# A graph layer's last turns reordered, its adjacency chunks kept in DRAM in 7 stripes

## The chip, the cores and the metric

The kernel runs on one core of a Trainium2 chip. The metric is device time in microseconds (us). Five engines work side by side: PE (TensorE: matmuls and transposes), DVE (VectorE), ACT (ScalarE), POOL (GpSimd) and SP (SyncE, which here only issues DMAs). Each runs its own program in order, and they wait on each other through semaphores. SP, ACT and POOL each have a DMA queue; all queues share the core's 16 DMA engines.

## The reference

Two graph layers over 6250 nodes (256 features) and 206250 edges, then a mixture of 8 experts (2 chosen per node). Cut to what matters:

```
norm = ew * rsqrt(deg_out[src] * deg_in[dst] + EPS)
h6   = relu(segment_sum((h5 @ W6)[src] * norm, dst) + b6)      # layer 1
h7   = relu(segment_sum((h6 @ W7)[src] * norm, dst) + b7)      # layer 2
x    = x + h7 @ Wp + bp
x    = x + moe(layernorm(x))      # gelu(xn @ W1[e] + b1[e]) @ W2[e] + b2[e], e = the top 2 of 8
```

The edges come sorted by `dst`.

## The kernel before

**Two ways to sum edges.** Edges are cut into tiles of 128. The first 736 tiles of layer 1 (784 of layer 2) are *dense*: 24 (26) chunks, for each of which an adjacency block of 49 x 128 rows by 134 columns is built in SBUF (`adj`, two buffers of 3283 KB) and multiplied by the whole feature table on PE (L2098, 49 matmuls a chunk). Layer 1 builds each block with DVE (`add_tile`, L1323) and SP stores it to DRAM (`store_chunk`, L763); layer 2 only loads it back (`load_chunk`, L768, for chunks 0 and 1 on ACT's queue, L1906). The DRAM tensor `chunks` holds 128 rows per chunk, one row of 26264 bytes for each partition.

The other tiles come in *groups* of 8, 110 in layer 1 and 104 in layer 2. POOL gathers the 8 x 128 source rows of a group from the layer's table in DRAM with 8 indirect DMAs (L977) into one of 4 ring buffers, and waits with a group until PE has summed the group 4 before it. PE sums a group (`sums`, L2111). After every second group ACT copies the sums (`copy_sums`, L1760), PE aligns them (`combine`, L2124), ACT copies the result (`copy_rows`, L1767), and SP adds the pair of groups to the node sums in DRAM (`store_group`, L740). Ahead of each odd group's `combine`, SP must have loaded one carried row (`carry_row`, L731), which was written by the store before. `store_group(L, n)` is the carried row's load for even n, and the store for odd n.

**Pairs.** Nodes are finished in 25 pairs of 128-row blocks. SP loads the pair's sums (`load_early`, L776), DVE scales them, PE transposes (L2133), ACT does the relu (L1805), PE projects (L2150), ACT scales (`pair_out`, L1814), and in layer 1 SP stores the rows to layer 2's table (`store_table`, L798). POOL begins layer 2's gathers only when all 25 pairs are in that table.

**The last turns of layer 1.** Groups 96 to 109 run in 14 turns (k = 0 to 13) of which each engine does its share in a written order. Pairs 9 to 22 are spread over turns 4 to 11 as 1, 2, 2, 2, 1, 2, 2, 2. In a turn PE does `sums`, dense steps and one-hot builds, all pairs of the turn, then `combine`; SP does the pairs' DMAs and then `store_group`. Pairs 23 and 24 follow behind turn 13. Turn 4 also issues `load_stored`, 2304 KB of the table back into SBUF; ACT issues a chunk store in turn 5 and a chunk load in turn 7.

**Layer 2's slots.** Each slot does one group and a third or a quarter of a chunk. From chunk 8 on every chunk has 4 slots and begins at an even slot, where SP issues the next chunk's load, a carried row of the dense sums, and then the group's carried row. A pair takes 6 slots (stages 0 to 5: transposes and `project`; residual and two normalisations on DVE, `residual_and_norms` L1369; router; places; the list, twice). `pair_starts` (L623) gives every pair its first slot, at least 3 apart; a pair whose rows end in a group can begin no sooner than slot `groups_for(1, b)` (L602). After slot 103 there are no more groups: slots 104 to `SLOTS` - 1 take two expert blocks each (`tail_slot`, L2260; 105 blocks in all), and DVE copies the experts' weights for them (`weights_at`, L1594, L1582) at the head of slots from 104 on. The other blocks follow in a plain loop.

Of the kernel before, what the change touches and what calls it, by code (L numbers as in the profile page):

```python
# [14 lines left out]
P = 128  # L15
# [40 lines left out]
OFFS, CHUNK_OFFS = 16, 32  # L56

# [27 lines left out]
def gnn_moe_kernel(nc, A):  # L85
# [37 lines left out]
    with ExitStack() as ctx:  # L123
# [16 lines left out]
        chunks = nc.dram_tensor("chunks", (ALL * P, XB_ALL * AWID), F32, kind="Internal").ap()  # L140
# [397 lines left out]

        def slice_bounds(i):
            return first_of_step(ZERO_BEHIND[i - 1] + 1) if i else 0, first_of_step(ZERO_BEHIND[i] + 1)  # L540


        LATE_PAIR = LOOP_PAIRS + 1
        TURNS = TAIL - TAIL_FROM - 2
        TAIL_PAIR_COUNT = LATE_PAIR - EARLY_PAIRS
        TAIL_PAIRS = [range(0)] * TAIL_FROM + [range(EARLY_PAIRS + TAIL_PAIR_COUNT * k // TURNS,
                                                     EARLY_PAIRS + TAIL_PAIR_COUNT * (k + 1) // TURNS)
                                               for k in range(TURNS)] + [range(0)] * 2
# [53 lines left out]
        def groups_for(L, b):  # L602
            return min(2 * ceil_div(tiles_before((b + 1) * PT * P) + 2 * TG - G0[L] * TG, 2 * TG), GROUPS[L])
# [71 lines left out]
        def _(sp):  # L675
# [87 lines left out]
            def store_chunk(c):  # L763
                sp.wait_ge(added, chunk_start(c + 1))
                sp.dma_start(chunks[c * P:(c + 1) * P, :], adj[:, c % 2].rearrange("p h w -> p (h w)")
                             ).then_inc(chunk_stored, 16)

            def load_chunk(c):  # L768
                sp.wait_ge(applied[1], SLICES * (c - 1))
                sp.dma_start(adj[:, c % 2].rearrange("p h w -> p (h w)"), chunks[c * P:(c + 1) * P, :]  # L770
                             ).then_inc(chunk_in[c % 2], 16)
# [50 lines left out]
            with sp.If(bad < 1):  # L822
# [39 lines left out]
                for k in range(TAIL):  # L862
                    if k == TAIL_FROM:
# [185 lines left out]
        def _(dve):  # L1049
# [600 lines left out]
            with dve.If(bad < 1):  # L1650
# [39 lines left out]
                for b in range(LATE_PAIR, NPAIR):  # L1690
                    tail_pair(b)
# [43 lines left out]
        def _(act):  # L1735
# [81 lines left out]
            def tail_pairs(pairs):  # L1817
                for b in pairs[:1]:
                    pair_root(b)
                for b in pairs:  # L1820
# [3 lines left out]
                    if b > EARLY_PAIRS:  # L1824
                        pair_out(b - 1)

# [79 lines left out]
            def load_chunk(c):  # L1906
                act.wait_ge(chunk_stored, 16 * (CHUNKS + c + 1))
                act.dma_start(adj[:, c].rearrange("p h w -> p (h w)"), chunks[c * P:(c + 1) * P, :]
# [574 lines left out]
```

## Time and profile before

| | us |
|---|---|
| median of 3 runs | 3170.95 (3157.32 to 3171.85) |
| the profiled execution, its own time | 3166.45 |
| its span, first to last instruction | 3164.5 |
| layer 1's gathers on POOL | 373.4 to 1520.0 |
| layer 2's gathers on POOL | 1555.3 to 2640.3 |
| PE / POOL / DVE busy | 83% / 62% / 60% of the span |

The profile lists for each engine its instructions with start, duration and, in brackets, how long the engine had been idle and what ended that. POOL's busy share leaves out the 0.30 us that it needs between two gathers.

### The profile page before, as it was taken

What the parts mean: (1) busy time and instruction counts of PE and PEld (TensorE: products, weight loads), DVE (VectorE), ACT (ScalarE), POOL (GpSimd) and SP (SyncE); (2) the same over time, 40 slices, a digit from 0 to 9 for tenths busy, and PEclk for the clock granted to TensorE, in tenths of its full rate; (3) what the DMA queues carried; (4) which work ended last, traced back from release to release, by engine and by line L of the source; (5) the groups of instructions that cost most, each with busy time, mean ns of one, the idle gap of its engine ahead of it and who ended that gap; (6) DMA issues with size and microseconds to landing.
All of it is one profiled execution on the core that took longest, in us unless ns stands there. A gap on an engine that the chain in (4) does not pass through costs nothing. (4 is left out here: it accounts for less than half of the span.)

```text
span 3164.5 us, 53882 instructions
## 1 busy us (share of the span) xinstructions
PE 2631.7 (83%) x16919; PEld 2013.0 (64%) x16919; DVE 1911.0 (60%) x6028; ACT 861.5 (27%) x2052; POOL 1963.4 (62%) x1932
## 2 busy tenths in 40 slices
PE   4567479999999999995589988888888875899995
PEld 3456247676667776663466766666666553889984
DVE  9999878888888887864203545455545446522210
ACT  5677611122121222112201100000011001456652
POOL 0000277777777777777477777777777763467763
PEclk8699789999999999997899999899999885999997
DMA  4001355566665655668666766666666663344444
GB/s 129 0 22 43 115 166 181 201 204 203 199 203 193 195 188 191 203 199 276 207 201 226 259 213 213 194 217 215 226 220 221 219 226 93 60 66 71 70 67 115
DMA packets 197506, 530.79 MB, mean 168 GB/s; under 512 B 39338, under 2 KB 129247, under 8 KB 190463
## 3 DMA queue, kind: packets, MB, share of 16 engines
q0 software_dynamic: 102336, 252.47, 30.5%
q1 hardware_dynamic: 92174, 256.65, 22.4%
q10 hardware_dynamic: 2736, 18.48, 1.5%
q8 instruction: 131, 2.15, 0.3%
q14 instruction: 129, 1.05, 0.1%
HBM read 377.61 MB, written 156.24 MB: 169 GB/s over the span
## 5 line engine op out<-in xcount | busy, mean ns | idle before, releaser
L977 POOL DMA_INDIRECT arena<-table,src_i x1712 | 1673.7, 978 | 596.2 <-issue 514.5
L2098 PE MATMUL bank<-arena 128*128 128x257 f32 x4900 | 1246.5, 391 | 3.1 <-ACT zcd L1784 2.4
L2098 PEld LDWEIGHTS bank<-arena 128*128 128x128 f32 x4900 | 901.7, 194 | 202.5 <-issue 83.4
L2083 PE MATMUL bank<-arena 128*128 128x294 bf16 x2352 | 426.2, 295 | 49.6 <-DVE arena L1295 32.3
L1323 DVE TENSOR_TENSOR arena<-arena,bank 128x294 f32 x784 | 357.3, 456 | 176.4 <-PE bank L2083 164.9
L1295 DVE SCALAR_TENSOR_TENSOR arena<-iota_f,arena 128x256 f32<-128x256 f32 x784 | 366.8, 468 | 0.0
L2083 PEld LDWEIGHTS bank<-arena 128*128 128x128 bf16 x2352 | 226.4, 100 | 207.9 <-DVE arena L1323 46.3
L2111 PE MATMUL bank<-arena,s_all 128*32 128x257 f32 x3424 | 246.2, 408 | 75.1 <-DMA arena<-table,src_i 68.4
L1771 ACT COPY arena<-zero 128x2144 f32<-128x2144 f32 (+1 forms) x104 | 156.3, 1533 | 398.3 <-DMA chunks<-arena 335.9
L1003 POOL DMA_INDIRECT acc<-arena x105 | 178.7, 1702 | 126.6 <-ACT arena L1897 97.6
L1294 DVE TENSOR_SCALAR arena<-iota_key,arena 128x294 bf16<-128x294 bf16 x784 | 242.7, 310 | 0.0
L2055 PE MATMUL bank<-arena 128*128 128x150 bf16 x1616 | 152.6, 256 | 107.6 <-DVE arena L1143 72.2
L1582 DVE COPY arena<-arena 128x1024 f32 x105 | 76.2, 733 | 261.9 <-PE bank L2297 245.7
L968 POOL PARTITION_ALL_REDUCE bad_all<-bad_f x1 | 0.4, 380 | 358.4 <-DVE bad_f L1285 358.4
L2055 PEld LDWEIGHTS bank<-arena 128*128 128x128 bf16 x1616 | 132.7, 109 | 128.9 <-DVE arena L1143 107.3
L2297 PE MATMUL bank<-arena 128*128 128x128 f32 x1680 | 211.0, 280 | 0.0
L2306 PE MATMUL bank<-arena 128*128 x840 | 203.1, 384 | 8.8 <-ACT arena L1897 8.8
L2111 PEld LDWEIGHTS bank<-arena,s_all 128*32 128x32 f32 x3424 | 93.5, 114 | 178.6 <-DMA arena<-table,src_i 76.1
L1760 ACT COPY zs<-bank 127x257 f32<-127x257 f32 x107 | 40.1, 375 | 608.2 <-PE bank L2111 607.3
L2297 PEld LDWEIGHTS bank<-arena 128*128 128x128 f32 x1680 | 202.2, 197 | 0.1
L2306 PEld LDWEIGHTS bank<-arena 128*128 128x128 f32 x840 | 153.3, 193 | 28.3 <-issue 10.5
L990 POOL DMA_INDIRECT arena<-rows_x,arena x105 | 109.2, 1040 | 85.1 <-DVE arena L1487 34.0
(238 smaller groups left out, 2678.3 us busy)
## 6 DMA issues: line engine op xcount, KB each, us to landing
chunks<-arena SPq DMA_DIRECT2D x25, 3283.0 KB, 12.7
arena<-chunks SPq DMA_DIRECT2D x24, 3283.0 KB
arena<-table,src_i POOLq DMA_INDIRECT x1712
zsum<-zc SPq DMA_DIRECT2D x107, 128.5 KB, 3.2
zrow<-zsum SPq DMA_DIRECT2D x50, 257.0 KB, 4.7
arena<-in_W ACTq DMA_DIRECT2D x16, 512.0 KB, 16.9
rows_x<-arena SPq DMA_DIRECT2D x25, 264.0 KB
arena<-chunks ACTq DMA_DIRECT2D x2, 3283.0 KB
```

Of the source, the lines that this page charges most:

```text
L977: pool.indirect_dma_start(gat[:, r, j, 0:D], None, table[L], bass.IndirectOffsetOnAxis(ap=src_i[:, col:col + 1], axis=0)).then_inc(gathere ...
L1003: pool.indirect_dma_start(acc, bass.IndirectOffsetOnAxis(ap=row_e[:, j:j + 1], axis=0), ye[:, j % 2], None, compute_op=ALU.add).then_inc(y ...
L1294: dve.tensor_scalar(ohk[:, r], iota_key[:, 0:KEYS], key[:, t:t + 1], None, ALU.is_equal)
L1295: dve.scalar_tensor_tensor(out=words[:, r], in0=bc_mid(iota_f[:, :], 2), scalar=lo_f[:, t:t + 1], in1=bc_in(w_words[:, t], P), op0=ALU.is_ ...
L1323: dve.tensor_tensor(win, win, ps_b[t % len(ps_b)].rearrange("p (h w) -> p h w", w=TW), ALU.add).then_inc(added, 1)
L1771: done = act.copy(adj[:, c % 2, first:first + whole], zero[:, :].unsqueeze(2).broadcast_to([P, whole, AWID]))
L2055: last = pe.matmul(ps_do, oh_lo[:, r, j // TI, :, j % TI], whi[:, r, j // TI, :, :, j % TI].rearrange("p i n -> p (i n)"), start=False, st ...
L2083: last = pe.matmul(ps_b[t % len(ps_b)], halves[:, t % OH_RING, word, :, half], ohk[:, t % OH_RING], start=(i == 0), stop=(i == 2))
L2098: last = pe.matmul(ps_ap, adj[:, c % 2, h, 0:P], xp[:, h], start=(h == 0), stop=(h == XB_ALL - 1))
L2111: last = pe.matmul(ps_seg[q * WIN:(q + 1) * WIN, :], s_mat[:, r, q * HQ + j], gat[:, r, q * HQ + j], start=(j == 0 and not second), stop=( ...
L2297: last = pe.matmul(ps_h[j % 2][:, c], w1_e[:, j % W1_RING, k, c * P:(c + 1) * P], xeT[:, j % 2, k], start=(k == 0), stop=(k == KD - 1))
L2306: last = pe.matmul(ps_y, hs[:, j % 2, c], w2_of(e, c), start=(c == 0), stop=(c == HC - 1))
```

## The change

Four things change.

1. `chunks` in DRAM gets 7 rows of 3752 bytes for each partition of a chunk in place of one of 26264; the same bytes are stored and loaded, each partition in 7 pieces.
2. In the last turns of layer 1 an odd turn's `combine`, `copy_rows` and `store_group` come behind the turn's first pair and no longer behind its last; an even turn's carried row is issued before the pairs.
3. Pair 23 (`LATE_PAIR`) is moved from behind turn 13 into turn 12; its projection comes ahead of the last group's `sums` on PE. One pair, 24, is left behind the last group.
4. For that, `groups_for` asks for 8 tiles of margin where it asked for 16. Layer 2's planner uses the same function. By its formula these first slots move, and the rest stay: pairs 14, 15, 16, 17 from 30, 38, 46, 54 to 28, 36, 44, 52; pair 23 from 104 to 102; pair 24 from 107 to 105. `SLOTS` goes from 113 to 111.

```diff
+STRIPES = 7
-        chunks = nc.dram_tensor("chunks", (ALL * P, XB_ALL * AWID), F32, kind="Internal").ap()
+        chunks = nc.dram_tensor("chunks", (ALL * STRIPES * P, XB_ALL // STRIPES * AWID), F32, kind="Internal").ap()
...
+        def striped(c):
+            return adj[:, c % 2].rearrange("p (k h) w -> p k (h w)", k=STRIPES)
+
+        def chunk_rows(c):
+            return chunks[c * STRIPES * P:(c + 1) * STRIPES * P, :].rearrange("(k p) n -> p k n", p=P)
...
         def groups_for(L, b):
-            return min(2 * ceil_div(tiles_before((b + 1) * PT * P) + 2 * TG - G0[L] * TG, 2 * TG), GROUPS[L])
+            return min(2 * ceil_div(tiles_before((b + 1) * PT * P) + TG - G0[L] * TG, 2 * TG), GROUPS[L])
...
-                                               for k in range(TURNS)] + [range(0)] * 2
+                                               for k in range(TURNS)] + [range(LATE_PAIR, NPAIR - 1), range(0)]
...
             def load_chunk(c):                                    # SP; ACT's and the stores likewise
                 sp.wait_ge(applied[1], SLICES * (c - 1))
-                sp.dma_start(adj[:, c % 2].rearrange("p h w -> p (h w)"), chunks[c * P:(c + 1) * P, :]
-                             ).then_inc(chunk_in[c % 2], 16)
+                sp.dma_start(striped(c), chunk_rows(c)).then_inc(chunk_in[c % 2], 16)
...
# SP, turn k
+                    if k == TAIL - 1:
+                        store_table(LATE_PAIR)
+                    if k % 2 == 0:
+                        store_group(0, LOOP_GROUPS + k)
                     for b in TAIL_PAIRS[k]:
+                        if b == LATE_PAIR:
+                            load_early(b)
                         if b + 2 < LATE_PAIR:
                             load_early(b + 2)
                         if b > EARLY_PAIRS:
                             store_table(b - 1)
-                    store_group(0, LOOP_GROUPS + k)
-                for b in range(LATE_PAIR, NPAIR):
-                    load_early(b)
-                for b in range(LATE_PAIR - 1, NPAIR):
-                    store_table(b)
+                        if k % 2 and b == TAIL_PAIRS[k][0]:
+                            store_group(0, LOOP_GROUPS + k)
+                    if k % 2 and not TAIL_PAIRS[k]:
+                        store_group(0, LOOP_GROUPS + k)
+                load_early(NPAIR - 1)
+                store_table(NPAIR - 1)
...
# PE, turn k
+                    if k == TAIL - 1:
+                        project(LATE_PAIR, 0, w7, ps_f(LATE_PAIR))
                     sums(0, n)
...
-                    for b in TAIL_PAIRS[k]:
+                    for b in TAIL_PAIRS[k][:1]:
                         tail_pair(b)
                     combine(0, n)
-                for b in range(LATE_PAIR, NPAIR):
-                    tail_pair(b)
+                    for b in TAIL_PAIRS[k][1:]:
+                        tail_pair(b)
+                pair_T(0, NPAIR - 1, (NPAIR - 1) % 2)
                 project(NPAIR - 1, 0, w7, ps_f(NPAIR - 1))
```

On ACT `copy_rows` moves behind the turn's first pair in the same way, `pair_out(23)` is done ahead of turn 13's `copy_sums`, and pair 24 alone follows behind.

## Rows read from the trace of the kernel before

**Rows 1.** Timeline of POOL between the layers (start us, us, instruction, [idle <-releaser])
```profile
1555.26 0.94 POOL L977 DMA_INDIRECT arena<-table,src_i  x1 [35.27 <-DMA table<-arena]
```
**Rows 2.** Timeline of PE, last turns of layer 1
```profile
1466.30 3.78 PE L2150 MATMUL bank<-w,hT 128*128 128x256 f32 x8 [16.62 <-ACT hT L1805]
...
1496.45 1.20 PE L2124 MATMUL bank<-zs,arena 128*128 128x257 f32 x2 [8.72 <-DMA zs<-zsum]
...
1520.63 1.08 PE L2111 MATMUL bank<-arena,s_all 128*32 128x257 f32 x16
...
1524.15 0.66 PE L2133 MATMUL bank<-ident,zr_all 128*128 128x128 f32 x4 [0.23 <-DVE zr_all L1362]
...
1528.08 0.60 PE L2124 MATMUL bank<-zs,arena 128*128 128x257 f32 x2
...
1535.41 1.20 PE L2124 MATMUL bank<-zs,arena 128*128 128x257 f32 x2 [4.86 <-DMA zs<-zsum]
...
1543.87 1.12 PE L2133 MATMUL bank<-ident,zr_all 128*128 128x128 f32 x4 [4.50 <-DVE zr_all L1362]
1545.91 3.40 PE L2150 MATMUL bank<-w,hT 128*128 128x256 f32 x8 [0.93 <-ACT hT L1805]
...
1550.68 1.99 PE L2150 MATMUL bank<-w,hT 128*128 128x256 f32 x8 [0.93 <-ACT hT L1805]
```
**Rows 3.** Timeline of SP's queue, the same stretch
```profile
1482.22 0.30 SPq L731 DMA_DIRECT2D zs<-zsum  x1
...
1534.04 0.30 SPq L731 DMA_DIRECT2D zs<-zsum  x1
...
1539.59 0.90 SPq L776 DMA_DIRECT2D zrow<-zsum  x2
```
**Rows 4.** Timeline of ACT's queue, turn 7
```profile
1480.50 0.36 ACTq L1908 DMA_DIRECT2D arena<-chunks  x1
```
**Rows 5.** DMA issues (size, median us to landing)
```profile
chunks<-arena SPq DMA_DIRECT2D x25, 3283.0 KB, 12.7
```
**Rows 6.** Windows (PE, PEld, DVE, ACT, POOL busy, granted clock, DMA share, GB/s)
```profile
850.00:853.00 3.00, 3.00 (x23) 2.16 (x16) 3.00 (x11) 0.00 (x0) 2.39 (x3) 1.00 0.99 421
...
875.00:891.00 16.00, 15.76 (x101) 11.46 (x98) 11.78 (x36) 4.03 (x9) 12.34 (x13) 1.00 0.43 126
```
**Rows 7.** Timeline of PE, start of layer 2
```profile
1570.26 1.94 PE L2111 MATMUL bank<-arena,s_all 128*32 128x257 f32 x16 [16.68 <-DMA arena<-table,src_i]
...
1615.47 1.94 PE L2111 MATMUL bank<-arena,s_all 128*32 128x257 f32 x16 [7.42 <-DMA arena<-table,src_i]
```
**Rows 8.** Waits in layer 2, 1616 to 2580 us (us in total, times, longest)
```profile
PE bank L2124 <- DMA zs<-zsum: 38.2, 17, 5.1
```
**Rows 9.** Timelines of SP's queue and of PE, a chunk load in layer 2
```profile
1880.34 0.42 SPq L770 DMA_DIRECT2D arena<-chunks  x1
...
1895.14 1.20 PE L2124 MATMUL bank<-zs,arena 128*128 128x257 f32 x2 [5.08 <-DMA zs<-zsum]
```
**Rows 10.** Timeline of PE, the last groups and the first expert blocks
```profile
2675.23 1.94 PE L2111 MATMUL bank<-arena,s_all 128*32 128x257 f32 x16
...
2683.44 3.62 PE L2297 MATMUL bank<-arena 128*128 128x128 f32 x16
...
2710.49 0.95 PE L2173 MATMUL bank<-arena 128*128 128x8 f32 x8
...
3088.98 1.95 PE L2297 MATMUL bank<-arena 128*128 128x128 f32 x16
...
3092.72 1.95 PE L2297 MATMUL bank<-arena 128*128 128x128 f32 x16
```
**Rows 11.** Timeline of DVE: one pair's stage 1, first and last; places, last
```profile
2646.53 0.68 DVE L1374 TENSOR_TENSOR arena<-bank,arena 128x512 f32<-128x512 f32 x1
...
2657.06 0.74 DVE L1119 TENSOR_SCALAR arena<-arena,mv,rv 128x256 f32<-128x256 f32 x2
...
2677.89 0.68 DVE L1491 TENSOR_TENSOR arena<-arena,bank 128x512 f32<-128x512 f32 x1
```

More of the change, by code:

```diff
@@ L602, in groups_for @@
         def groups_for(L, b):
-            return min(2 * ceil_div(tiles_before((b + 1) * PT * P) + 2 * TG - G0[L] * TG, 2 * TG), GROUPS[L])
+            return min(2 * ceil_div(tiles_before((b + 1) * PT * P) + TG - G0[L] * TG, 2 * TG), GROUPS[L])
+        LATE_PAIR = LOOP_PAIRS + 1
+        TURNS = TAIL - TAIL_FROM - 2
+        TAIL_PAIR_COUNT = LATE_PAIR - EARLY_PAIRS
+        TAIL_PAIRS = [range(0)] * TAIL_FROM + [range(EARLY_PAIRS + TAIL_PAIR_COUNT * k // TURNS,
+                                                     EARLY_PAIRS + TAIL_PAIR_COUNT * (k + 1) // TURNS)
+                                               for k in range(TURNS)] + [range(LATE_PAIR, NPAIR - 1), range(0)]
+        assert LATE_PAIR == NPAIR - 2 and groups_for(0, LATE_PAIR) == GROUPS[0] - 2
         PAIR_IN_CHUNK = {chunks_for(b) + 1: b for b in range(EARLY_PAIRS)}
@@ L764, in store_chunk @@
                 sp.wait_ge(added, chunk_start(c + 1))
-                sp.dma_start(chunks[c * P:(c + 1) * P, :], adj[:, c % 2].rearrange("p h w -> p (h w)")
-                             ).then_inc(chunk_stored, 16)
+                sp.dma_start(chunk_rows(c), striped(c)).then_inc(chunk_stored, 16)
             def load_chunk(c):
                 sp.wait_ge(applied[1], SLICES * (c - 1))
-                sp.dma_start(adj[:, c % 2].rearrange("p h w -> p (h w)"), chunks[c * P:(c + 1) * P, :]
-                             ).then_inc(chunk_in[c % 2], 16)
+                sp.dma_start(striped(c), chunk_rows(c)).then_inc(chunk_in[c % 2], 16)
             def load_pair(L, b, slot, turn, made):
@@ L1689, in _ @@
                         tail_pair(b)
-                for b in range(LATE_PAIR, NPAIR):
-                    tail_pair(b)
+                tail_pair(NPAIR - 1)
                 next_matrix(1, 0)
@@ L1815, in pair_out, with tail_pairs @@
                 last.then_inc(p_out, 1)
-            def tail_pairs(pairs):
+            def tail_pairs(pairs, n):
                 for b in pairs[:1]:
@@ L1825, in tail_pairs @@
                         pair_out(b - 1)
+                    if b == pairs[0]:
+                        copy_rows(0, n)
+                if not pairs:
+                    copy_rows(0, n)
             def features_T(i):
@@ L1907, in load_chunk @@
                 act.wait_ge(chunk_stored, 16 * (CHUNKS + c + 1))
-                act.dma_start(adj[:, c].rearrange("p h w -> p (h w)"), chunks[c * P:(c + 1) * P, :]
-                              ).then_inc(chunk_in[c], 16)
+                act.dma_start(striped(c), chunk_rows(c)).then_inc(chunk_in[c], 16)
             def load_experts():
@@ L1989, in _ @@
                     n = LOOP_GROUPS + k
+                    if k == TAIL - 1:
+                        pair_out(LATE_PAIR)
                     copy_sums(0, n)
@@ L1998, in _ @@
                         act.wait_ge(added, DT + LATE_CT[0])
-                        act.dma_start(chunks[CHUNKS * P:(CHUNKS + 1) * P, :], adj[:, CHUNKS % 2].rearrange("p h w -> p (h w)")
-                                      ).then_inc(chunk_stored, 16)
+                        act.dma_start(chunk_rows(CHUNKS), striped(CHUNKS)).then_inc(chunk_stored, 16)
                     if k == FIRST_LOADED_AT:
                         load_chunk(0)
-                    tail_pairs(TAIL_PAIRS[k])
-                    copy_rows(0, n)
-                tail_pairs(range(LATE_PAIR, NPAIR))
+                    tail_pairs(TAIL_PAIRS[k], n)
+                pair_root(NPAIR - 1)
+                pair_relu(0, NPAIR - 1, b6c)
                 pair_out(NPAIR - 1)
@@ L2361, in _ @@
                     n = LOOP_GROUPS + k
+                    if k == TAIL - 1:
+                        project(LATE_PAIR, 0, w7, ps_f(LATE_PAIR))
                     sums(0, n)
```

7 lines of the change are left out of this document (removed).

## The prediction

> **What bounds the kernel now.** I read the page first (busy shares by slice), then POOL's gathers, then the timelines of PE, SP and ACT where POOL stands still, then the waits of layer 2 and the last slots.
>
> Layer 1's loop is bound by POOL: 880 gathers from 373.4 to 1520.0 us, one each 1.30 us, and hardly a wait for a buffer. What PE waits there costs nothing. Then POOL stands still for 35.3 us until the last pair is in the table [rows 1]: this gap is what parts 2 and 3 of the change aim at. In layer 2 a gather and its gap take 0.95 + 0.30 = 1.25 us, so 832 of them need 1040 us, and they take 1085: the rest is POOL waiting for a ring buffer, that is for PE. After the wait at 1615 us [rows 7] PE waits for gathered rows no more, so from there PE sets the pace, and its own waits count: the dearest is for the carried row, 17 times, 38.2 us [rows 8]. From 2580 us on DVE's serial work sets the pace, and from the first expert blocks on it is PE, 3.74 us a block [rows 10].
>
> **The end of layer 1: the new order.** Before, turn 11 begins at 1520.63, its combine comes at 1528.08 behind both pairs, its sums are stored and the next carried row leaves at 1534.04 (5.96 later), the last combine follows at 1535.41, pairs 23 and 24 are loaded from 1539.59, and POOL starts at 1555.26 [rows 1 to 3]. The new combine of turn 11 stands behind the first pair's transposes (1524.15 + 0.66), so at 1524.8, 3.3 earlier, and the sums have landed at 1530.8. But now pair 23 lies ahead of the last group's sums on PE: load to transposes 4.3 (1539.59 to 1543.87), to the projection 2.0, the projection 2.0 to 3.4 (both in [rows 2]; I take 2.7), the last sums 1.1 and ACT's copy and the wait for it about 1: with 0.4 for the issue, 11.5. So the last combine comes at 1542.3, not at 1535.4. Behind it one pair less is left: 1555.26 - 1535.41 = 19.9, less the distance of the two projections, 4.8, makes 15.1. Restart at 1557.4. **By itself the new order is worth -2 us, from +1 to -4 (a loss):** what it takes from behind the last group it puts ahead of it, and nothing else fills the time, as that group's rows have long landed. The carried row issued ahead of the pairs saves nothing where PE comes to it late anyway; SP's pair loads behind its wait are hidden by two turns of lead.
>
> **The end of layer 1: the stripes.** PE is late in turn 11 because two things were stuck. One row of 1 KB issued at 1482.22 lands at 1496.4, 14 us later, with ACT's chunk load of 1480.50 in flight, and PE stands 8.7 us for it [rows 2 to 4]; likewise 16.6 us at 1466.30, behind ACT's chunk store and `load_stored`. A chunk takes 12.7 us to land [rows 5] and fills the engines meanwhile: share 0.99 at 421 GB/s, against 0.43 at 126 with gathers alone [rows 6]. With pieces of 3.7 KB a small transfer of another queue waits for one piece and not for 26 KB, if the engines take turns by pieces. I take all of the 8.7 us, and 1 of the 16.6, since there SP's own 2304 KB stand ahead of the pair's load in the same queue. The bound is what turn 11 can gain at all: its group's rows were gathered 16 gathers before the last, at about 1500, and land 5.3 later as those of layer 2's first group do (1565.0 to 1570.26, [rows 7]), so 1520.6 - 1505 = 15.6. 9.5 less 2 is **7.5 us faster** for the restart, between 13 faster and 4 slower.
>
> The Trainium skill (DMA: Bandwidth & Descriptors, Queues, rings and completion order) says that each engine goes round its queue rows and drains a whole packet of one before it switches, in order within a row. It speaks for the stripes if a piece is a packet and against them if a packet holds many; by the first the 8.7 us go, by the second nothing does and the restart is 2 us later. The 14 us of the carried row fit either.
>
> **The start of layer 2.** Group 4's rows land 7.4 us late, in a chunk load's shadow [rows 7]; as PE sets the pace after that, what the stripes take from this wait is kept. I take 5 of 7.4, and 1 of group 0's: **6 faster**, between 8 and 0.
>
> **The middle of layer 2.** Here the chunk load and the carried row are in one queue, SP's, and the row is issued right behind: load at 1880.34, row landed at 1895.14, 14.8 us, PE waiting 5.1 [rows 9]. It lands with the chunk. So stripes can't let it pass, and if they give the gathers their full share, the chunk lands later. By how much: gathers alone hold the engines 0.43 of the time. A chunk that got only the other 0.57 would take 3283 KB at 0.57 x 421 = 240 GB/s, 14 us, and with 2 of latency (an estimate) 16, against 12.7: 3.3 later. 17 waits x 3.3 = 56 us is the upper end, 0 the lower. Nearer to a size is this: 10.7 us at 421 GB/s move 4.5 MB, of which the chunk is 3.4; the gathers want 126 x 10.7 = 1.35 MB and so lack only some 0.25 MB, which at their own 126 / 0.43 = 293 GB/s is 0.85 us. With a little for 56 pieces an engine in place of 8 I take 1.1 us a wait: **19 us slower**. A gain isn't excluded: a chunk that landed earlier could return up to 38. Pairs 14 to 17, two slots earlier, put their first stage (3.4 us of PE work) ahead of the combine that waits, and take their third away from the next: no sum.
>
> **The end of layer 2.** This comes with `groups_for`. Pair 23's stage 1 is 11.3 us of DVE in one piece (2646.53 to 2657.80, [rows 11]). Before, it ran in slot 105, beside expert blocks whose weights DVE had already copied. Now it runs in slot 103, ahead of DVE's first weight copies of slot 104, and PE has no blocks and no groups left to do. Its transposes and projection (slot 102) also stand ahead of the last group's sums: DVE's copies and places of slot 102 end at 2678.5 [rows 11]; scaling 0.6, transposes 1.1, relu 0.9 and projection 3.4 (as behind the idle stretch of [rows 2]) make 2684.5, the norms 2696.1 with their wait, the weight copy 2696.8. The first block begins there and not at 2683.44 [rows 10]: 13.4 later. PE then does block 0 (3.6), list 1.5, transposes 0.9, block 1 (4.2), router product 1: pair 23's router product is done at 2708.0, before at 2711.4 (2710.49 + 0.95). 3.4 earlier, but with 2 blocks behind it and not 6: 4 x 3.74 = 15.0, less 3.4. **12 us slower**, between 7 and 15. From there on both run alike, and PE has no cover to hide it: the block loop keeps it busy to the end.
>
> **Sum.** -7.5 - 6 + 19 + 12 = +17.5 us on the profiled execution, 3166.5. That execution is 4.5 below the median of the runs, so I add the sum to the median: 3170.95 + 17.5 = 3188. Layer 1's loop adds nothing: chunk stores that land 1 to 3 us later delay ACT's zeroing, which has the rest of a 41 us chunk.
>
> **Rivals.**
> - *The stripes change nothing* (the engines take turns by longer runs than a piece): no gain at 1496 and at 1615, no later chunks. +2 + 12 = 3185. The trace doesn't exclude it: a chunk of 8 pieces an engine and one of 56 were never side by side. Chance 0.15.
> - *Stripes free the small transfers and chunks land when they did:* -10 - 8 + 0 + 12 = -6, 3165. For it: the gathers lack only 0.25 MB at a chunk's end, so little is there to be given back. Chance 0.2.
> - *Faster:* chunks land earlier in pieces, and the carried row behind them with it. The price is 17 x the time saved, up to 38: -10 - 8 - 38 + 12 = -44, 3127. It decides from 0.6 us a chunk on (17 x 0.6 = 10 and the 6 above make 16, that is 0.5%). Against it: the engines are already at a share of 0.99. Chance 0.13.
> - *Chunks pay in full:* 3.3 us each. -7 - 6 + 50 + 12 = 3220. Chance 0.08.
> - My forecast has the remaining 0.44, with its own range of 3178 to 3208.
>
> **How the numbers follow.** About 0.5% (16 us) is what a measurement of this kernel can tell from no change, so "slower" begins at 3187 and "faster" below 3155. Slower: two thirds of the forecast (0.30), half of the first rival (0.07), the last (0.08) = 0.45. Faster: 0.13, and a quarter of the second = 0.18. Same: 0.37. The range must reach from the second rival to the upper part of the forecast: 3157 to 3214 leaves out most of the faster rival and part of the last.
>
> **What the new profile would show.** POOL's restart near 1548 (1557 if the stripes do nothing); PE's 8.7 us wait at 1496 gone; chunk stores landing in 13.5 to 15 us, against 12.7; packets up by 51 x 768 = 39,000; the waits of PE for the carried row up from 38 to some 57 us; POOL waiting more in layer 2; the first expert block some 14 us further behind the last gather, and the plain loop of blocks with four more blocks in it. I am wrong most easily in the price of a chunk, which counts 17 times: 1 us of it is half of the whole sum.

## The result and the profile after

The changed kernel takes 3251.43 us (median; 3244.39 to 3255.37), the kernel before in the same measurement 3171.40: a ratio of 1.0257 [1.0218, 1.0296], or 81 us slower (the ratio times 3164 us, about the time of the kernel before). The forecast of 3188 and its range of 3157 to 3214 both lie too low. The profiled execution took 3255.01 us with a span of 3252.9, 88.4 more than before.

The end of layer 1, by POOL's timeline (the restart, as in [rows 1]) and PE's (the last combine and the last pair, as in [rows 2]; L2142 is before's L2124, L2151 its L2133, L2168 its L2150):

```profile
1570.40 0.94 POOL L992 DMA_INDIRECT arena<-table,src_i  x1 [41.28 <-DMA table<-arena]
```
```profile
1554.34 0.70 PE L2142 MATMUL bank<-zs,arena 128*128 128x257 f32 x2 [0.49 <-ACT zs L1774]
...
1562.27 1.11 PE L2151 MATMUL bank<-ident,zr_all 128*128 128x128 f32 x4 [7.23 <-DVE zr_all L1377]
1564.32 3.50 PE L2168 MATMUL bank<-w,hT 128*128 128x256 f32 x8 [0.93 <-ACT hT L1819]
...
1595.82 1.08 PE L2129 MATMUL bank<-arena,s_all 128*32 128x257 f32 x16 [1.26 <-DMA arena<-table,src_i]
...
1625.81 1.94 PE L2129 MATMUL bank<-arena,s_all 128*32 128x257 f32 x16 [4.15 <-DMA arena<-table,src_i]
```

The restart is 15.1 us later than in [rows 1]. The 8.7 us for a carried row in layer 1 are gone, and the wait of 7.42 at the start of layer 2 ([rows 7]) is now one of 1.26, one of 4.15 and a third of 3.45 at 1656.

DMA issues of the page, size and median us to landing. A stored chunk lands after 14.8 us and not after 12.7 ([rows 5]):

```profile
chunks<-arena SPq DMA_DIRECT2D x25, 3283.0 KB, 14.8
arena<-chunks SPq DMA_DIRECT2D x24, 3283.0 KB, 16.3
...
arena<-chunks ACTq DMA_DIRECT2D x2, 3283.0 KB, 19.1
```

Waits of PE from 1616 to 2580 us (total, times, longest), as in [rows 8], and then the window itself, of the changed kernel and of the one before (columns as in [rows 6]):

```profile
PE bank L2142 <- DMA zs<-zsum: 68.2, 14, 9.3
PE bank L2151 <- DVE zr_all L1377: 23.3, 10, 8.8
PE bank L2230 <- DVE off_i L1475: 22.3, 5, 7.0
```
```profile
1616.00:2580.00 964.00, 802.66 (x4514) 602.42 (x4513) 415.67 (x1844) 84.89 (x223) 669.62 (x701) 0.91 0.66 206
```
```profile
1616.00:2580.00 964.00, 847.86 (x4874) 637.20 (x4870) 457.11 (x2009) 92.09 (x241) 713.24 (x747) 0.94 0.67 215
```

In the same 964 us PE does 360 matmuls fewer (4514 and 4874 in the first pair of brackets). It stands longer for the carried row, and the granted clock falls from 0.94 to 0.91.

POOL's waits for PE in layer 2 (1550 to 2800 us), changed kernel and then the one before:

```profile
POOL arena L992 <- PE bank L2129: 111.7, 33, 10.8
```
```profile
POOL arena L977 <- PE bank L2111: 41.6, 17, 12.2
```

This row turned out to be the one to read. From POOL's first to last gather of layer 2, less these waits, it is 1037 to 1047 us in all 20 kernels (before 1043.5, after 1038.6). What PE, DVE or a DMA loses costs time only as far as it arrives in this row. The phase grew from 1085.1 to 1150.3 us: 65 of the 88 us. Of the rest 9 us are the last gather of layer 1 (1520.0 to 1529.1), 6 the gap behind it, 14 the way from the last gather to the first expert block, less 6 that the rest of the kernel takes less.

The first expert block begins 57.4 us behind the last gather (2720.7), before 43.1 ([rows 10]), so 14.3 later, close to the 13.4 of the forecast:

```profile
2778.14 3.78 PE L2315 MATMUL bank<-arena 128*128 128x128 f32 x16 [7.99 <-DVE arena L1597]
```

### The profile page after: what moved, and what is told of

The parts are those of the page before. It is cut to its first block and busy times, and to the rows that moved or that the text cites. A ratio compares the mean times of both kernels' runs of the same rounds, so it can differ in the third digit from the quotient of the medians.

```text
span 3252.9 us, 53876 instructions
## 1 busy us (share of the span) xinstructions
PE 2653.8 (82%) x16919; PEld 2023.7 (62%) x16919; DVE 1907.3 (59%) x6030; ACT 859.2 (26%) x2052; POOL 1959.8 (60%) x1932
## 2 busy tenths in 40 slices
DMA packets 237440, 530.79 MB, mean 163 GB/s; under 512 B 39337, under 2 KB 129246, under 8 KB 237054
## 5 line engine op out<-in xcount | busy, mean ns | idle before, releaser
L1774 ACT COPY zs<-bank 127x257 f32<-127x257 f32 x107 | 39.9, 372 | 592.7 <-PE bank L2129 592.2
## 6 DMA issues: line engine op xcount, KB each, us to landing
chunks<-arena SPq DMA_DIRECT2D x25, 3283.0 KB, 14.8
arena<-in_W ACTq DMA_DIRECT2D x16, 512.0 KB, 16.6
```

## The experiments

Eighteen kernels ran. The us are the ratio times 3164; the last column is POOL's waits for PE in layer 2, in the profiled execution.

| kernel | ratio [interval] | us | POOL waits |
|---|---|---|---|
| before | | | 41.6 |
| changed | 1.0257 [1.0218, 1.0296] | +81 | 111.7 |
| e1 stripes only | 1.0160 [1.0122, 1.0198] | +51 | 99.3 |
| e2 planner only | 1.0131 [1.0093, 1.0169] | +41 | 64.1 |
| e3 order only | 1.0008 [0.9989, 1.0027] | +3 | 37.1 |
| e4 stripes and order | 1.0141 [1.0102, 1.0180] | +45 | 90.2 |
| e5 carried row ahead of the load | 1.0021 [1.0003, 1.0040] | +7 | 45.8 |
| e6 the same, with stripes | 1.0063 [1.0040, 1.0086] | +20 | 73.3 |
| e7 pairs 23, 24 early | 1.0037 [1.0010, 1.0064] | +12 | 36.7 |
| e8 pairs 14 to 17 early | 1.0096 [1.0068, 1.0123] | +30 | 65.7 |
| e9 49 stripes | 1.1382 [1.1348, 1.1417] | +437 | 186.2 |
| e10 load in parts | 1.0047 [1.0021, 1.0073] | +15 | 50.7 |
| e11 the same, pairs as e8 | 0.9988 [0.9964, 1.0013] | -4 | 32.5 |
| e12 e8, load in slot 2 | 0.9900 [0.9877, 0.9924] | -32 | 13.1 |
| e13 load in slot 2 | 0.9902 [0.9877, 0.9928] | -31 | 10.3 |
| e14 load in slot 1 | 1.0395 [1.0373, 1.0417] | +125 | 166.7 |
| e15 the same, with stripes | 1.0429 [1.0405, 1.0454] | +136 | 183.2 |
| e16 changed, load in slot 2 | 0.9944 [0.9926, 0.9963] | -18 | 11.0 |
| e17 stripes, load in slot 2 | 0.9946 [0.9926, 0.9966] | -17 | 35.9 |
| e18 order, load in slot 2 | 0.9914 [0.9896, 0.9931] | -27 | 13.9 |

### The four parts one by one (e1 to e4)

e1 is the kernel before with the diff's `STRIPES`, `striped` and `chunk_rows` alone. e2 and e3 split `groups_for` by the layer; e3 has the new order of the last turns besides, and e4 is e3 with the stripes:

```diff
 # e2
-            ... + 2 * TG - G0[L] * TG ...
+            ... + (1 if L else 2) * TG - G0[L] * TG ...
 # e3 and e4: as changed, but
-            ... + TG - G0[L] * TG ...
+            ... + (2 if L else 1) * TG - G0[L] * TG ...
 # e3
-STRIPES = 7
+STRIPES = 1
```

> The kernel before with the chunks in 7 stripes and nothing else. Theory (each part has its own price, the stripes' being chunks that land 2 to 3 us later with a carried row behind them): +25 us, from +15 to +40; chunk stores land in 14.8 us, PE's waits for the carried row in layer 2 go from 38 to 60 or 70 us, the wait of 8.7 us near 1496 is gone. Rival (the stripes do nearly all of the +80): +60 to +80. Rival (the stripes do nothing by themselves, the planner's new slots do it all): within 8 us of before.

> The kernel before with layer 2's first slots alone moved (margin of 8 tiles for layer 2, 16 for layer 1; last turns and chunks as before). Theory: +12 us from pair 23's normalisations ahead of the first expert block, and 0 to +15 in slots 28 to 60, where pairs 14 to 17 now have their work ahead of one chunk's combine and none ahead of the next: +12 to +27. Rival (stripes do it all): within 8 us of before. Rival (the planner does it all): +50 or more. First expert block 55 to 60 us behind the end of the gathers, against 43.

> The last turns of layer 1 in the new order (pair 23 in turn 12, combines behind the first pair), chunks whole, layer 2's slots as before. Theory: the restart of the gathers comes 2 us later than before, from 1 earlier to 4 later, and nothing else changes: -1 to +5 us. Rival (the new order itself adds the 6 us that the gap has grown by, and more): +6 to +12.

> The changed kernel with layer 2's first slots put back (stripes and new last turns stay). Theory (parts add up): the stripes' price and the order's, +20 to +45 us, some 40 us below the changed kernel. Rival (stripes do it all): +70 to +80. Rival (the planner does it all): within 8 us of before.

Measured +51, +41, +3 and +45: e1 and e2 lie above the ranges that I gave, e3 and e4 within theirs. Stripes, planner and order add up to 95 against 81 for the whole, as far as such intervals (some 12 us each) can tell. So each part has a price of its own, and two of them are far above what I gave them.

### The carried row taken out of the load's shadow (e5, e6)

```diff
                     if c and j == 0:
+                        if g is not None and g % 2 == 0:
+                            store_group(1, g)
                         store_rows(1, c - 1)
                         if c + 1 < ALL:
                             load_chunk(c + 1)
                         carry_chunk(1, c)
-                    if g is not None:
+                    if g is not None and not (c and j == 0 and g % 2 == 0):
                         store_group(1, g)
```

> The kernel before, with one move in SP's queue: at the first slot of each chunk of layer 2 the carried row of that slot's group is fetched ahead of the store of the last chunk's sums and of the load of the next chunk, in place of behind them. My theory (the row is late because it stands behind 3.3 MB in its own queue): most of the 38.2 us of waits go, and with them part of the clock that PE loses by standing still (0.94 granted in the middle of layer 2); 25 to 55 us faster, 3110 to 3140. Rival (the row is late because all 16 DMA engines are full for 12 us, whichever queue it comes by): the row then leaves some us before the chunk anyway, so the waits go in this kernel too, but only where SP isn't held by its wait for the last group's store; where SP is held (9.1 us at the longest) the chunk load leaves later by as much and PE then waits for the chunk: 0 to 15 us faster. A third: POOL's gathers are the true bound within a few us of PE (1.25 us each), and the gain stops at some 20 us as the waits turn up as PE waits for gathered rows.

> As e5, but with the chunks in 7 stripes. The stripes alone cost 49 us: the waits for the carried row rose from 38 to 71 us, the rest seems to be PE's clock (0.94 to 0.92 granted between 1616 and 2580) and thus a consequence. If that chain is right, then with the row ahead of the chunk load the stripes cost next to nothing: this kernel within 12 us of e5. Rival (striped loads hurt by themselves: PE waits for the chunk, or for gathers that the stripes slow): it stays 25 to 50 us behind e5, and the waits of PE show another line, the chunk or gathered rows.

I missed e5: +7 us, not 25 to 55 faster. PE's groups in e5, 1616 to 2580 us (busy, mean ns | idle before and its releaser):

```profile
L2126 PE MATMUL bank<-zs,arena 128*128 128x257 f32 x92 | 27.9, 385 | 0.0
...
L2135 PE MATMUL bank<-ident,zr_all 128*128 128x128 f32 x84 | 17.5, 342 | 52.8 <-DVE zr_all L1364 52.8
```

Of the 38.2 us of waits for the carried row nothing is left, and those for the scaled pair rows have grown from 23.4 to 52.8: DVE in its turn waits for `zrow<-zsum`, 130.9 us in that window where it was 88.6. The wait passed to the next small load in the same shadow: over layer 2's gathers PE stands still for 172.4 us in e5 and for 174.9 before. e6 came out 13 us behind e5, just outside the 12 that I had allowed. Between e5 and e6 the stripes cost 13 us, and 51 where the carried row stands behind the load: most of their price goes through that row.

### The planner's two halves (e7, e8)

```diff
 # e7: pairs 23 and 24        # e8: pairs 14 to 17
-            ... + 2 * TG - G0[L] * TG ...
+            ... + (1 if L and b > 22 else 2) * TG - G0[L] * TG ...
+            ... + (1 if L and b < 20 else 2) * TG - G0[L] * TG ...
```

> The kernel before with the smaller margin for pairs 23 and 24 of layer 2 alone (starts in slots 102 and 105, not 104 and 107; pairs 14 to 17 stay at 30, 38, 46 and 54). By my prediction's working this part costs 12 us (7 to 15): the first expert block 13 us later behind the last gather, two slots and four blocks fewer under the pairs' stages. Rival (all of the 36 us that both together cost come from the end): 30 to 36 us slower, and the middle of layer 2 as before.

> The kernel before with the smaller margin for pairs 14 to 17 of layer 2 alone (starts in slots 28, 36, 44 and 52, not 30, 38, 46 and 54; pairs 23 and 24 stay). My prediction costed this at nothing. The trace of the kernel with both parts speaks for 24 us between slots 28 and 60: in slots 32, 40, 48 and 56, where a chunk load is in flight, the pair's third stage used to stand ahead of the combine that waits for the carried row, and now nothing does. If so: 18 to 28 us slower, 3182 to 3192, with the longest waits for the carried row at those four slots. Rival (the middle's loss in that trace was scatter): 0 to 5 us.

e7 costs 12 us, as forecast; its first block comes 57.4 us behind the last gather, as in the changed kernel, 14.3 more than before, forecast 13.4. e8 costs 30; both together are 42, and e2, which has both, measured 41. Its reason in my expectation was wrong, though: the waits for the carried row only change places (39.9 us in e8, 38.2 before). What is new is on DVE. SP's queue and DVE in e8, around two chunk loads:

```profile
2013.69 0.44 SPq L770 DMA_DIRECT2D arena<-chunks  x1
...
2018.42 0.42 SPq L776 DMA_DIRECT2D zrow<-zsum  x1
...
2054.72 0.42 SPq L770 DMA_DIRECT2D arena<-chunks  x1
...
2061.82 0.47 SPq L819 DMA_DIRECT2D acc<-arena  x1
```
```profile
2029.27 0.76 DVE L1362 TENSOR_SCALAR zr_all<-zrow,mv 128x256 f32<-128x256 f32 x2 [10.08 <-DMA zrow<-zsum]
...
2072.94 0.69 DVE L1374 TENSOR_TENSOR arena<-bank,arena 128x512 f32<-128x512 f32 x1 [9.29 <-DMA acc<-arena]
```

A pair's rows are loaded 4.7 us behind a chunk load and a pair's result is stored 7.1 us behind the next one. Both take 11 us, and DVE stands idle for 9 to 11 of them, four times for the rows and three times for the result between 1870 and 2300 us. These are not transfers of the moved pairs: they belong to the pairs that begin between them (slots 33, 41, 49, 57), and before they leave as close behind a load, the rows 5.1 us and the result 8.0 (at 2059.37). What the move changed is when DVE needs them. Before, DVE has work of the pair ahead and comes to the rows at 2020.83 without a wait; and the next pair, whose `residual_and_norms` must wait for that result to be stored, begins in slot 46 and not in 44, so nothing waits for it. The result that DVE does need at once, of the pair that began in slot 38, leaves 21.5 us behind a load:

```profile
2002.85 0.42 SPq L770 DMA_DIRECT2D arena<-chunks  x1
...
2007.98 0.42 SPq L776 DMA_DIRECT2D zrow<-zsum  x1
...
2024.36 0.54 SPq L819 DMA_DIRECT2D acc<-arena  x1
```
```profile
2020.83 0.61 DVE L1362 TENSOR_SCALAR zr_all<-zrow,mv 128x256 f32<-128x256 f32 x2
...
2030.12 0.69 DVE L1374 TENSOR_TENSOR arena<-bank,arena 128x512 f32<-128x512 f32 x1 [6.52 <-DMA acc<-arena]
```

The changed kernel shows e8's pattern whole (11.01 us idle for `acc` at 2008.07, 10.97 for `zrow` at 2056.95).

### What a piece costs (e9)

```diff
-STRIPES = 7
+STRIPES = 49
```

> The stripes alone, with 49 in place of 7: pieces of 0.5 KB, 392 an engine and chunk, where 7 stripes have 56 and the kernel before 8. In windows of 2 us inside a chunk's transfer the 16 engines are at a share of 1.0 in both kernels, but move 420 to 446 GB/s with 8 pieces and 380 to 400 with 56, and a chunk takes 2.1 us longer to land. Theory: each piece costs the engine time of its own, some 40 ns (2.1 us by 48 more pieces). Then 384 more pieces make a chunk land about 17 us later (28 to 32 us in all), the windows show 200 to 240 GB/s at a full share, and the kernel is much slower: over 200 us. Rival (my prediction's: the stripes only let the gathers have their share): landing can't go beyond 16 us, at 56 or at 392 pieces alike, and the kernel is within 20 us of that with 7 stripes (3213).

Windows inside a stored chunk's transfer, of the kernel before, of e1 and of e9:

```profile
512.20:520.20 8.00, 8.00 (x57) 5.79 (x55) 7.81 (x25) 0.00 (x0) 6.17 (x7) 1.00 1.04 414
```
```profile
512.50:520.50 8.00, 8.00 (x56) 5.79 (x55) 7.81 (x25) 0.00 (x0) 6.17 (x7) 1.00 1.02 398
```
```profile
583.00:599.00 16.00, 11.13 (x72) 7.93 (x70) 7.57 (x24) 0.00 (x0) 12.34 (x13) 0.93 1.18 241
```

The engines are full in all three, and with more pieces they move fewer bytes. From a store's issue to ACT's zeroing that waits for it are 12.9 us with 8 pieces an engine, 14.8 with 56 and 28.4 with 392 (medians): 1.9 us for 48 more and 15.5 for 384 more, 40 ns a piece by both, as I had expected. The row behind a load comes 13.0, 15.5 and 19.2 us after the load's issue, that is 2.5 us for 48 more and 6.2 for 384.

That both stores give 40 ns is a coincidence, though, and not a price of a piece. The trace has every packet that the engines moved; each piece is one (197,506 packets before, 237,440 in the changed kernel: 52 transfers of 768 more pieces). Here are one chunk load before ([rows 9]) and one in e1, from the load's first packet to its last, 11.65 and 13.07 us (queue: packets, MB, share of the 16 engines; q1 is SP's queue, q0 POOL's gathers):

```profile
q1 hardware_dynamic: 163, 3.35, 79.1%
q0 software_dynamic: 264, 0.75, 17.8%
```
```profile
q1 hardware_dynamic: 916, 3.36, 71.3%
q0 software_dynamic: 479, 1.32, 28.9%
```

The load's own packets keep an engine busy for 9.2 and 9.3 us. What makes it 1.4 us longer are the gathers, which take 2.1 and 3.8 us of every engine's time and move 0.75 and 1.32 MB. The means over all transfers of SP's queue (us of an engine's time; MB of the gathers meanwhile):

| | first to last packet | own packets | gathers | gathers' MB |
|---|---|---|---|---|
| 25 stores: before, e1, e9 | 10.2, 12.1, 25.7 | 8.20, 8.55, 20.04 | 1.8, 3.2, 8.9 | 0.66, 1.18, 2.55 |
| 24 loads: before, e1, e9 | 11.4, 14.0, 18.2 | 8.84, 9.36, 13.15 | 2.0, 3.6, 5.6 | 0.69, 1.30, 1.71 |

While a whole chunk is in flight the gathers get about 60 GB/s, and with 7 stripes or 49 some 95. So with 7 stripes it is my prediction's mechanism that makes a chunk land later: it leaves the gathers more of the engines. A piece by itself costs 7 ns (stores) to 11 (loads). With 49 stripes it costs 31 and 11 (at most, as packet times overlap there: a share of 1.18), and it is the stores' own packets that do most. The landing goes far beyond the rival's 16 us, so the gathers' share isn't all of it there; with 7 stripes it is most of it, 1.5 of 1.9 us in a store and 1.7 of 2.5 in a load. Most of the 437 us lie in layer 1, where ACT's late zeroing makes POOL wait 335.3 us for PE.

### Where the load stands (e10 to e15)

e10 cuts each load into two or three parts, one a slot, behind that slot's `store_group`; e11 has the early pairs of e8 besides. PE waits for the sum of the parts.

```diff
-            def load_chunk(c):
-                sp.wait_ge(applied[1], SLICES * (c - 1))
-                sp.dma_start(adj[:, c % 2].rearrange("p h w -> p (h w)"), chunks[c * P:(c + 1) * P, :]
-                             ).then_inc(chunk_in[c % 2], 16)
+            def load_chunk(c, k):
+                if k == 0:
+                    sp.wait_ge(applied[1], SLICES * (c - 1))
+                lo, hi = (XB_ALL * AWID * i // parts_of(c) for i in (k, k + 1))
+                sp.dma_start(adj[:, c % 2].rearrange("p h w -> p (h w)")[:, lo:hi],
+                             chunks[c * P:(c + 1) * P, lo:hi]).then_inc(chunk_in[c % 2], 16)
```

> The kernel before, each chunk load of layer 2 cut into three (two for the chunks of three slots) column parts of 1.1 MB, issued in successive slots behind that slot's store of sums or carried row; layout as before, pieces of 8.9 KB. Theory (what costs is that for 12 us all 16 engines are full, and whatever small load PE needs next in that time is late: in the kernel before the carried row, with the row moved ahead the pair's rows): no shadow is longer than 4 to 5 us, most of the 38.2 us of waits for the carried row and some of the 23.4 us for the pair's rows go, the clock in the middle of layer 2 rises from 0.94: 20 to 50 us faster. Rival (POOL's 1.25 us a gather bounds layer 2 just behind PE, or the waits spread over three slots in place of one): 0 to 10 us either way.

> e10 with pairs 14 to 17 of layer 2 two slots earlier, as in e8. Those alone cost 29 us with whole chunk loads. Theory (they cost because their stages no longer stand ahead of the combine in the slots where a chunk load is in flight): with the load spread over the slots there is no such slot, and this kernel is within 10 us of e10. Rival (the pairs' own DVE work collides in their new slots, whatever the loads do: PE's longest waits for the one-hots rose from 3.6 to 5.8 us): it stays 20 us or more behind e10.

Both missed. e10 is 15 us slower: no wait for the carried row is left, but PE's for DVE's one-hots grew from 10.8 to 42.7 us and DVE's for `acc<-arena` from 49.6 to 80.2. Yet PE stands no longer than before, 172.5 us over layer 2's gathers against 174.9: what is longer is its busy time with the same matmuls, 924.0 us against 910.1, at a granted clock of 0.89 against 0.91. That every slot now has a short shadow is my reading of it, not shown. In e11 the early pairs are 19 us better than in e10, where with whole loads they were 30 us worse. So neither place of the pairs is good in itself; what counts is how they stand to the chunk loads.

e13 moves the whole load two slots on, e12 does that in e8, and e14 puts it into the second slot behind the store (e15: with stripes):

```diff
                         store_rows(1, c - 1)
-                        if c + 1 < ALL:
+                        if c + 1 < ALL and SPANS[c] < 4:
                             load_chunk(c + 1)
                         carry_chunk(1, c)
+                    if c and j == 2 and SPANS[c] == 4 and c + 1 < ALL:
+                        load_chunk(c + 1)
                     if g is not None:
                         store_group(1, g)
```
```diff
 # e14, e15: nothing in the first slot, and
                     if g is not None:
                         store_group(1, g)
+                    if c and j == 1 and c + 1 < ALL:
+                        load_chunk(c + 1)
```

> e8 (pairs 14 to 17 two slots earlier, starts in the first slot of a chunk) with the chunk load issued two slots later too, in the third slot of each chunk of four slots, ahead of that slot's carried row. Pairs and loads so stand to each other as in the kernel before, and both are moved against the chunks' borders. Theory (what e8 lost, 29 us, is the place of the pairs' work against the load): within 8 us of the kernel before, 3157 to 3172. Rival (it is the place of the pairs against the chunk's first slot, with the waits of DVE and PE there, or the pairs against each other): it stays at e8's 3190, within 8.

> The kernel before with the chunk load alone two slots later, as in e12; pairs as before. By the theory of e12 pairs and loads stand to each other as in e8: some 20 to 30 us slower, 3184 to 3195, with POOL's waits for PE in layer 2 at 60 to 70 us in place of 42. By its rival: within 8 us of the kernel before.

> The kernel before with the chunk load of layer 2 issued in the second slot of each chunk, behind that slot's store of sums: no carried row is due in that slot, and the next one leaves some 10 us later. POOL's gathers and their gaps make 1043 us of layer 2 in every kernel so far, and POOL's waits for PE are added to that, so there are 42 us to be had at most, of which 12 at the end of the layer come from DVE. Theory (the load's 12 us shadow costs what falls into it): the waits for the carried row fall under 10 us and the kernel is 10 to 25 us faster. Rival (seen in e5 and e10: with the row in time PE waits as long for the pairs' rows or for DVE's one-hots): within 5 us of the kernel before.

> e14 with 7 stripes. With the load ahead of the row the stripes cost 49 us, with the row ahead of the load 17 to 20. If all that the stripes do is to lengthen each load's shadow by 2 to 3 us (7 more pieces for each of 8, at a full share of the engines), then here, where nothing is due at its end, they cost under 10 us against e14. Rival (the stripes slow the gathers or something else all along): 17 us or more.

I had e12, e13 and e14 wrong, theory and rival alike, and they settled the cause; e15, 11 us behind e14, lies between its theory (under 10) and its rival (17). I had counted only where pairs begin; but each pair has two transfers that DVE waits for, its rows in its first slot and its result in its fourth. Before, pairs 14 to 17 begin in a chunk's third slot and pairs 3 to 6 between them in the second, so rows go out in slots 2 and 1 and results in slots 1 and 0 (slots counted from 0). A load in slot 1, behind the store, has the result of slot 1 and the rows of slot 2 right behind it. SP's queue and DVE in e14:

```profile
2063.35 0.42 SPq L770 DMA_DIRECT2D arena<-chunks  x1
...
2064.34 0.46 SPq L819 DMA_DIRECT2D acc<-arena  x1
...
2114.06 0.42 SPq L770 DMA_DIRECT2D arena<-chunks  x1
2116.66 0.39 SPq L776 DMA_DIRECT2D zrow<-zsum  x1
```
```profile
2080.19 0.69 DVE L1374 TENSOR_TENSOR arena<-bank,arena 128x512 f32<-128x512 f32 x1 [17.32 <-DMA acc<-arena]
...
2129.98 0.84 DVE L1362 TENSOR_SCALAR zr_all<-zrow,mv 128x256 f32<-128x256 f32 x2 [11.52 <-DMA zrow<-zsum]
```

Each costs DVE its whole landing, and all together cost the kernel 125 us. A load in slot 2 stands behind that slot's rows, and no rows or results follow before the next chunk: between 1870 and 2300 us no result and no row load of e13 leaves less than 22 us behind a load. SP's queue and POOL's waits in e13:

```profile
2010.63 2.40 SPq L819 DMA_DIRECT2D acc<-arena  x1
2013.08 0.46 SPq L770 DMA_DIRECT2D arena<-chunks  x1
...
2043.37 0.42 SPq L819 DMA_DIRECT2D acc<-arena  x1
...
2050.40 0.37 SPq L776 DMA_DIRECT2D zrow<-zsum  x1
...
2051.34 0.46 SPq L770 DMA_DIRECT2D arena<-chunks  x1
```
```profile
POOL arena L979 <- PE bank L2113: 10.3, 9, 6.8
```

POOL gathers nearly without a stop, and the kernel is 31 us faster than before. With the load there, the pairs' places no longer count (e12 -32, e13 -31).

### The change with the load in slot 2 (e16 to e18)

The same diff as e13's, in the changed kernel, in e1 and in e3.

> The changed kernel whole (stripes, new order, pairs 14 to 17 and 23 to 24 early) with the chunk load in the third slot of the chunks of four slots. Theory: what the change costs in the middle of layer 2 is what falls into the load's shadow, and in that place nothing does. The load place took 33 us from the kernel before (e13) and 64 from e8 (e12), and with it the middle pairs' place no longer counted. So POOL's waits for PE in layer 2 fall from 112 to under 30 us; what stays is the last pairs' 9 us and the 3-slot chunks with stripes: 3126 + 9 + 5 to 15 = 3140 to 3155, some 100 us faster than the changed kernel as it is. Rival (the stripes and the early pairs each have a cost of their own beside the shadow): 33 us faster than the changed kernel and no more, 3210 to 3220.

> The stripes alone (e1: 49 us with the load in the first slot, 12 in the second slot with everything late) with the load in the third slot. Theory: they only lengthen the shadow by 2 to 3 us; there they cost 0 to 12 us against e13, 3126 to 3138. Rival (a cost of their own for each load): 3150 and more.

> The new order of layer 1's last turns alone (e3: ratio 1.0008) with the load in the third slot, as the version of all parts that may be the best. By e3 the order is worth nothing: 3120 to 3132, within 0.3% of e13. If the order was hidden before by what followed, it would show here as 5 us or more.

e16 came out as the theory said: 3144.91 us, 3% below the changed kernel as it is (0.9944 to 1.0257), and POOL's waits are 11.0 in place of 111.7. PE still waits 33.4 us for the carried row in it and the kernel loses nothing by that, as POOL sets the pace. The stripes keep a price of some 14 us here (e17 to e13), a little above what I expected. In the profiled executions it goes through the carried row again, which slot 2's load has behind it: PE waits 48.8 us for it in e17 and 8.1 in e13, and POOL's waits are 35.9 and 10.3. e16 is only 9 us above e18, with the stripes and the early last pairs (12 us in e7) in it, so nothing is left for the stripes there. The order is worth nothing (e18 to e13, within the intervals). The best version is e13, or e12: 1.0% faster than the kernel before.

## Why the prediction was wrong

Two steps carry the miss: pairs 14 to 17, which I put at nothing (30 us), and the stripes in the middle of layer 2, which I sized at 19 us (51 in e1, with the gains that I had expected and that did not come). Each step by its own name:

- **The new order, 2 slower: right.** e3 measured +3, with an interval of -3 to +9. In e3 and e18, which have the order without stripes, the last combine of layer 1 is at 1545.0 and 1539.1 (forecast 1542.3) and POOL restarts at 1561.0 and 1555.4 (forecast 1557.4). Ten kernels with the layer 1 of before restart between 1551.4 and 1560.8, on average at 1555.3, so one profile doesn't tell such a step. The changed kernel restarted at 1570.4, and e4 and e16, with the same layer 1, at 1557.2 and 1558.3: of its 15 us later restart I claim none for the change.
- **The stripes at the end of layer 1, 9.5 gained: mechanism right, gain wrong.** (8.7 and 1 make 9.7.) The carried row of [rows 3] landed 14.2 us behind its issue ([rows 2]); in the ten kernels with this order and whole chunks it took 11.7 to 14.4, in the four with 7 stripes 8.0 to 9.2. So small transfers of another queue do pass between the pieces. But the restart is 1555.2 on average with stripes alone (four kernels) and 1555.3 without (ten). In e1 PE waits 3.1 us for the row and not 8.7, yet it comes to it 6.2 us later: 3.4 us late already in turn 3, ahead of `load_stored`, and later still behind a wait of 18.1 in place of the 16.6 at 1466. Behind the row it loses 2.4 us more, 1.1 of them waiting for DVE. I had counted a wait that went as time that came back. The Trainium skill (DMA: Bandwidth & Descriptors, Queues, rings and completion order) says that an engine changes queue rows between packets; the trace agrees with it, as here each piece is a packet: 14.2 to 8.7 us.
- **The start of layer 2, 6 faster: wrong.** PE waits 25.0 us for gathered rows there before ([rows 7] and one wait of 0.91) and 25.1 in e1; what one group waited less the next ones waited more.
- **The middle of layer 2, 19 slower by the stripes: the largest term, the mechanism right, the size less than half.** I let the gathers have their share, at 1.1 us a chunk, and the packets show just that, at 2.5. I had the gathers lack 0.25 MB, because I took the 421 GB/s of 3 us of a store ([rows 6]) for the whole of a load; the load of [rows 9] moves 352 GB/s from its first packet to its last, and the gathers moved 0.6 MB more in e1. PE's waits for the row went from 38.2 to 70.8 us. And a second price was not in the sum: PE needs longer for the same matmuls. PE, from the first to the last gather of layer 2, before and in e1 (columns as in [rows 6]):

```profile
1555.26:2640.30 1085.04, 910.14 (x5197) 680.67 (x5197) 491.70 (x2165) 99.19 (x260) 795.12 (x832) 0.91 0.68 221
```
```profile
1558.57:2694.60 1136.03, 926.72 (x5196) 693.19 (x5197) 488.56 (x2165) 99.04 (x260) 792.59 (x832) 0.90 0.66 211
```

  The phase is 51.0 us longer, 34.4 of them standing and 16.6 busy, at a lower granted clock. My rival that chunks pay in full had +50 for this and a chance of 8%; it is the same mechanism with 3.3 us a chunk, and its number fits in part by luck, as it had waits alone in it.
- **Pairs 14 to 17, "no sum": the step that failed outright, 30 us.** I weighed PE's 3.4 us of stage work and not the pairs' DMAs. With the two slots DVE comes at once to rows and results that leave right behind chunk loads, where before it had other work or no need of them: 9 to 11 us each.
- **The end of layer 2, 12 slower: right,** e7 measured 12.
- **Sum.** With the measured prices, 3 + 51 + 30 + 12 = 96, against 81 measured; in place of -7.5 - 6 + 19 + 12.

What stays open: why a piece of 0.5 KB costs 31 ns in a store and 11 in a load; why PE's clock is lower in e10 with no more waits; and whether small transfers do better on another queue than the chunk load's. In layer 2 all that I moved stands behind the load in SP's own queue, so the runs there don't part "behind it in the queue" from "the engines are full". Only layer 1's row, on another queue than the load, does: it is late with whole chunks and passes with stripes.

## What to carry to other kernels

A large transfer that fills all DMA engines for 12 us casts a shadow: what leaves in it lands at its end (with pieces of 26 KB whichever queue it comes by, with pieces of 3.7 KB in the same queue). List what each queue issues within that time, loads and stores that an engine waits for alike, and put the transfer where nothing of it is needed soon; here that was a move by two slots, worth 31 us, and the wrong slot cost 125. When a step is moved by a slot, its DMAs, and the time at which their results are needed, move against such a transfer too. And before pricing a wait, look for the one row to which it must come (here POOL's waits for PE): 38 us of waits taken away gave nothing, as the next wait took their place.

## What the hardware showed that I had not expected

- Large transfers and gathers that meet on full engines share them by the size of their pieces: beside a chunk in pieces of 26 KB the gathers move about 60 GB/s, beside pieces of 3.7 or 0.5 KB some 95, and the chunk pays for it, landing 2 to 2.5 us later. In all, the full engines move 414 GB/s beside pieces of 26 KB, 398 beside 3.7 KB and 241 beside 0.5 KB.
- Where PE stands much it is slower as well. The same two combine matmuls take 1.20 us behind a wait of 4.86 and 0.60 without one ([rows 2]), at granted clocks of 0.50 and 1.00, the lower and the upper of the clock's two levels (1.2 and 2.4 GHz). Over layer 2's gathers PE stands for 174.9, 209.3 and 260.7 us (before, e1, e14), the granted clock is 0.91, 0.90 and 0.85, and the same matmuls keep it busy for 910, 927 and 946 us. The sum of the waits doesn't say it all: in e10 PE stands for 172.5 us and has a clock of 0.89.
